# Part of level 0 moved beside the count matrix, the final sum scaled at its end, full-row bias products and a different last wait, in a graph and expert kernel

## The reference

```python
x = x + gnn(layernorm(x), src, dst)          # 625 nodes x 256, 20000 edges
x = x + ffn(layernorm(x))                    # 8 experts, the 2 best of each node, hidden size 512
# gnn: three levels, then one product over all of them
xs = [x]; h = x
for W, b in ((W0, b0), (W1, b1), (W2, b2)):
    m = concatenate([h[dst], h[src] - h[dst]]) @ W + b
    s = segment_sum(m, dst); cnt = segment_sum(1, dst)
    h = relu(s / maximum(cnt, 1)); xs.append(h)
return concatenate(xs) @ Wf + bf
```

## Time and profile before

| | us |
|---|---|
| median of three runs | 203.26 (201.93 to 204.81) |
| the profiled execution, its own time | 204.21 |
| its span | 202.4 |
| TensorE matmuls busy | 164.4 (81%) |
| VectorE busy | 100.7 (50%) |
| ScalarE busy | 70.3 (35%) |
| GpSimd busy | 69.8 (34%) |
| mean granted clock | 0.913 |

### The profile page before, as it was taken

One profiled execution on the slowest core, in us unless ns is written; L12 is line 12 of the kernel. 1 busy time (PEld: TensorE's weight loads), 2 busy tenths in 40 slices (PEclk: granted clock), 3 DMA queues, 4 the chain that ended last, 5 costly groups with the idle time before them and its releaser, 6 DMA issues.

```text
span 202.4 us, 3153 instructions
## 1 busy us (share of the span) xinstructions
PE 164.4 (81%) x1013; PEld 135.6 (67%) x1014; DVE 100.7 (50%) x259; ACT 70.3 (35%) x199; POOL 69.8 (34%) x96
## 2 busy tenths in 40 slices
PE   0443575877999999999999889996999999999700
PEld 0332354766899788989899879983676677657500
DVE  7799988784660447224534876922232232223100
ACT  7234984551400136112421076013334343433200
POOL 8506910003029075002000200005555666564560
PEclk9999995585579999999999996999999999999975
DMA  5469999500000501000000179902143235432332
GB/s 144 158 165 378 367 366 368 193 0 5 3 3 0 159 5 47 7 3 3 0 3 0 48 199 279 375 32 78 11 69 80 52 52 71 77 63 26 53 52 26
DMA packets 15784, 20.34 MB, mean 100 GB/s; under 512 B 1482, under 2 KB 12116, under 8 KB 15636
## 3 DMA queue, kind: packets, MB, share of 16 engines
q1 hardware_dynamic: 12420, 15.75, 24.2%
q0 software_dynamic: 2544, 3.54, 10.5%
q10 hardware_dynamic: 800, 0.79, 1.1%
HBM read 16.81 MB, written 3.26 MB: 99 GB/s over the span
## 4 chain that ended last, share of the span: by engine, by line
PE 66%; DVE 13%; DMA 7%; issue 4%; ACT 4%; POOL 2%; ACTq 1%; POOLq 0%; DVEq 0%
PE cnt_ps L1639 9%; PE bank L1620 5%; PE bank L1487 5%; PE cnt_ps L1338 5%; PE g_ps L1620 4%; DMA out_rows<-y_sb,row_put 4%; PE cnt_ps L1487 4%; PE bank L1331 3%; PE g_ps L1331 3%; PE g_ps L1332 3%; PE g_ps L1333 3%; DVE hot_lo L950 2%; PE bank L1333 2%; PE bank L1332 2%; DVE a_hi L1030 2%
## 5 line engine op out<-in xcount | busy, mean ns | idle before, releaser
L1639 PE MATMUL cnt_ps<-w_sb,h_t 128*128 x104 | 24.8, 381 | 2.7 <-ACT h_t L859 2.7
L1639 PEld LDWEIGHTS cnt_ps<-w_sb,h_t 128*128 128x128 f32 x104 | 18.7, 190 | 5.2 <-issue 3.2
L623 POOL DMA_INDIRECT out_rows<-y_sb,row_of x10 | 15.9, 1586 | 15.5 <-DMA out_rows<-y_sb,row_of 11.6
L617 POOL DMA_INDIRECT xg<-x_rows,row_of x12 | 12.0, 1003 | 23.4 <-DVE row_of L1297 20.1
L1379 PE MATMUL bank<-hot_key,hot_lo 125*128 125x45 bf16 (+4 forms) x80 | 8.3, 244 | 12.8 <-DVE hot_key L953 7.9
L1379 PEld LDWEIGHTS bank<-hot_key,hot_lo 125*128 125x128 bf16 x80 | 5.3, 124 | 15.4 <-DVE hot_key L953 13.2
L1273 DVE TENSOR_TENSOR y_sb<-cnt_ps,b_bc 128x256 f32<-128x256 f32 x13 | 5.5, 425 | 20.0 <-PE cnt_ps L1639 20.0
L950 DVE TENSOR_TENSOR hot_lo<-iota_lo,edge_rel 125x1024 bf16<-125x1024 int16 x20 | 14.2, 710 | 0.9 <-PE g_ps L1379 0.7
L1338 PE MATMUL cnt_ps<-ident 128*128 128x128 f32 x100 | 13.5, 297 | 0.0
L1620 PE MATMUL bank<-w_sb,xt 128*128 x28 | 13.4, 599 | 0.1
L1338 PEld LDWEIGHTS cnt_ps<-ident 128*128 128x128 f32 x100 | 12.9, 211 | 0.0
(11 more groups left out here) (279 smaller groups left out, 433.9 us busy)
## 6 DMA issues: line engine op xcount, KB each, us to landing
w_sb<-in_L_ffn_W SPq DMA_DIRECT2D x16, 512.0 KB, 10.2
b_bc<-in_L_ffn_b SPq DMA_DIRECT2D x8, 256.0 KB, 5.3
w_stage<-in_L_gnn_W SPq DMA_DIRECT2D x3, 512.0 KB, 5.6
w_stage<-in_L_gnn_Wf SPq DMA_DIRECT2D x4, 256.0 KB, 6.4
b_bc<-in_L_ffn_b SPq DMA_DIRECT2D x1, 1024.0 KB, 12.3
x_rows<-x_f ACTq DMA_DIRECT2D x1, 640.0 KB, 8.7
x_sb<-in_x SPq DMA_DIRECT2D x1, 512.0 KB
out_rows<-x_sb SPq DMA_DIRECT2D x1, 512.0 KB
```

The costliest lines, as they stand in the source:

```text
L617: pool.indirect_dma_start(out=xg[:, b, :], out_offset=None, in_=x2_rows, in_offset=bass.IndirectOffsetOnAxis(ap=rows, axis=0)).then_inc(x_ ...
L623: pool.indirect_dma_start(out=out, out_offset=bass.IndirectOffsetOnAxis(ap=rows, axis=0), in_=y_sb[:, b, :], in_offset=None, compute_op=AL ...
L1639: last = pe.matmul(bank[3][:, 0:D], h_t[:, k, :], w2_sb[:, ds(e, 1), k, :], start=k == 0, stop=k == HC - 1)
```

## The change

- In the count stage, ScalarE no longer makes `ht_f`. TensorE computes the own part of level 0 from unscaled h (`own0_product`, four parts, six products each) between the pairs; ScalarE takes it out with b0 added (`own0_out`, into `z0`; b0 comes as columns by a transfer of its own). `ys_lower` moves ahead of later pairs and additions.
- Level 0: after the degrees TensorE runs the gathered sums, then the bias and `g_product(0)` of the final sum. VectorE multiplies `z0` by the counts, adds the gathered sums and makes the lower parts. The products that spread rdeg go.
- The final sum: levels 1 to 3 add unscaled u @ Wf; level 0's part and x are added into x1 first, and the sum over u is multiplied by 1/deg when it is added. relu(u) * rdeg and its split go. `add_h` stands ahead of the gathered sums in levels 1 and 2. `Z_ORDER` and `YS_ORDER` become plain order.
- Bias products use 128 rows, the others zero. b0 is no more among them.
- `split_weights(1)` no longer waits for rdeg. `split_weights(2)` and (3) wait for `g_added` too.
- SyncE itself waits for the last scatter.

The diff, cut to its core:

```diff
-        b_rows = sb("b_rows", [BR, D], f32, gnn)
+        b_rows = sb("b_rows", [P, D], f32, gnn)
...
+            sp.dma_start(b0_col[:], B[0].rearrange("(k p) -> p k", k=KC), allow_slow_non_contiguous=True)\
+                .then_inc(b0_in, 16)
...
-            sp.wait_ge(all_scattered, 1)
+            sp.wait_ge(experts_ready, 2)
+            more = pairs(sp)
+            is_odd = odd_tile(sp)
+            for h in range(2):
+                sp.wait_ge(x_got[h], more * 16 + 16)
+            sp.wait_ge(scattered, more * 32 + is_odd * 16 + FIXED * 16)
+            sp.sem_inc(all_scattered, 1)
...
-            pool.wait_ge(rdeg_ready, 2)
             split_weights(1)
...
-                act.copy(ht_f[:, c, a:b], xn_bank(i)).then_inc(h0_copied, 1)
+            def own0_out(i):
+                cols, c = part(i)
+                act.wait_ge(own0_ps, i + 1)
+                act.activation(z0[:, c, cols], own0_bank(i), ACT.Identity, bias=b0_col[:, c:c + 1])\
+                    .then_inc(own0_ready, 1)
...
             hot_pair(16)
+            ys_lower(0, 1)
             hot_pair(17)
-            ys_lower(0, 1)
+            ys_lower(0, 2)
             add_halves(0, SPLIT_CHUNK)
-            ys_lower(0, 2)
             hot_pair(18)
+            ys_lower(0, 3)
             hot_pair(19)
-            ys_lower(0, 3)
+            ys_lower(0, 4)
             add_halves(1, CHUNKS)
-            ys_lower(0, 4)
...
+            for i in range(4):
+                scale_own0(i)
+            add_gathered(0)
+            mark(dve.tensor_tensor(diag[:], cnt_f[:].rearrange("p (t m) -> p t m", t=NT),
+                                   ident[:].unsqueeze(1).broadcast_to((P, NT, P)), ALU.mult))
+            add_gathered(1)
+            ut_lower(0, 0)
+            ut_lower(0, 1)
+            add_gathered(2)
+            wait_marked()
+            mark(dve.tensor_reduce(deg_col[:], diag[:], AX.X, ALU.add))
+            add_gathered(3)
+            ut_lower(0, 2)
+            ut_lower(0, 3)
...
+            for t in range(NT):
+                dve.tensor_tensor(x1_sb[:, t, :], g_tile(t), x_sb[:, t, :], ALU.add).then_inc(x_added, 1)
...
+                dve.scalar_tensor_tensor(x1_sb[:, t, :], g_tile(t), rdeg_col[:, t:t + 1], x1_sb[:, t, :],
+                                         ALU.mult, ALU.add).then_inc(x1_ready, 1)
...
+            sum_pair(28)
             ys_product(0, 1)
+            own0_product(0)
+            sum_pair(30)
             ys_product(0, 2)
+            sum_pair(32)
             pe.wait_ge(ys_ready, 1)
+            own0_product(1)
+            pe.wait_ge(ys_ready, 2)
             ys_product(0, 3)
+            sum_pair(34)
+            pe.wait_ge(own0_ready, 1)
+            own0_product(2)
+            sum_pair(36)
+            pe.wait_ge(ys_ready, 3)
             ys_product(0, 4)
+            sum_pair(38)
+            pe.wait_ge(own0_ready, 2)
+            own0_product(3)
...
-            for t in range(NT):
-
-                pe.matmul(g_tile(t), row_pick[:, LEVELS, :], b_split[:], start=t % 2 == 0, stop=False,
-                          skip_group_check=True)
-            for t in range(NT):
-                last = g_product(0, t)
-            last.then_inc(g_added, 1)
...
-                pe.matmul(z_bank(i), bias[:, l, m], cnt[:, cols], start=first, stop=False, skip_group_check=True)
+                pe.matmul(z_bank(i), bias[:, l - 1, m], cnt[:, cols], start=True, stop=False, skip_group_check=True)
...
                     pe.wait_ge(ys_ready, l * NT + 3)
-                    own_part(l, 1, bias, cnt, True, False)
+                    own_part(l, 3, bias, cnt)
+                    pe.wait_ge(x_added, NT)
+                    add_h(l)
                     pe.wait_ge(ys_ready, (l + 1) * NT)
-                    own_part(l, 0, bias, cnt, True, False)
-                    for i in (2, 3):
-                        gathered_sum(l, i, y_parts, a_t, False, True)
-                    if l < LEVELS - 1:
-                        add_h(l)
-                    for i in (0, 1):
-                        gathered_sum(l, i, y_parts, a_t, False, True)
+                    own_part(l, 2, bias, cnt)
+                    for i in range(4):
+                        gathered_sum(i, y_parts, a_t, False)
```

More of the change, by code:

```diff
@@ L1359, in ys_product, with own0_product, g_product @@
                 last.then_inc(ys_done, 1)
-            def g_product(l, t, hi=ht_hi, lo=ht_lo):
+            def own0_product(i):
+                cols, c = part(i)
+                m = slice(D + c * P, D + (c + 1) * P)
+                for k in range(KC):
+                    last = exact3(own0_bank(i), (w_hi[:, 0, k, m], w_lo[:, 0, k, m]),
+                                  (ht_hi[:, k, cols], ht_lo[:, k, cols]), k == 0, k == KC - 1)
+                last.then_inc(own0_ps, 1)
+            def g_product(l, t, hi, lo, first=False):
                 r, cols = l % 2, slice(t * P, (t + 1) * P)
@@ L1406, in _, with sum_pair @@
                 last.then_inc(xn_t_done, 1)
-            for u in range(20, 28):
+            def sum_pair(u):
                 sum_unit(u)
+                sum_unit(u + 1)
+            for u in range(20, 28, 2):
+                sum_pair(u)
             pe.wait_ge(w_split, 1)
@@ new lines, in level_sums @@
+                        gathered_sum(i, y_parts, a_t, True)
+                else:
+                    pe.wait_ge(ut_ready, 4 * (l - 1) + 2)
+                    own_part(l, 0, bias, cnt)
+                    own_part(l, 1, bias, cnt)
+                    for t in range(NT):
+                        if t == 1:
+                            pe.wait_ge(ut_ready, 4 * l)
+                        if t >= 3:
+                            pe.wait_ge(ys_ready, l * NT + t - 2)
+                        ys_product(l, t)
@@ L1557, in _ @@
                     pe.wait_ge(w_split, l + 1)
+                if l == 1:
+                    pe.wait_ge(cnt_read, 2)
                 with pe.If(is_general > 0):
-                    level_sums(l, [ys_hi[:].bitcast(f32), ys_lo[:].bitcast(f32)], a_f, b_level[:].bitcast(f32),
-                               cnt_f[0:BR, :])
+                    level_sums(l, [ys_hi[:].bitcast(f32), ys_lo[:].bitcast(f32)], a_f, b_level[:].bitcast(f32), cnt_f)
                 with pe.Else():
                     level_sums(l, [ys_hi, ys_lo], a_hi, b_level, cnt_r)
-            add_h(LEVELS - 1)
+                if l == 0:
+                    pe.wait_ge(b_ready, 2 + (LEVELS - 1))
+                    pe.wait_ge(own0_ready, 4)
+                    for t in range(NT):
+                        pe.matmul(g_tile(t), row_pick[:], b_split[:], start=t % 2 == 0, stop=False, skip_group_check=True)
+                    for t in range(NT):
+                        last = g_product(0, t, ht_hi, ht_lo)
+                    last.then_inc(g_added, 1)
             pe.wait_ge(w_split, LEVELS + 1)
-            for j, t in enumerate(YS_ORDER):
-                if j in (0, 2):
-                    pe.wait_ge(ht_ready, 4 * LEVELS + (4 if j else 2))
+            for t in range(NT):
+                if t in (0, 3):
+                    pe.wait_ge(ut_ready, 4 * LEVELS - (0 if t else 2))
                 g_product(LEVELS, t, ut_hi, ut_lo).then_inc(g_done, 1)
```

284 lines of the change are left out of this document (108 added, 176 removed).

## The result

| | before | after |
|---|---|---|
| median beside each other, four runs each | 204.03 us (201.93 to 205.23) | 185.30 us (185.05 to 187.13) |
| the profiled execution, its own time | 204.21 | 185.45 |
| its span | 202.4 | 183.5 |

The ratio is 0.912 (95% interval 0.908 to 0.917): faster by 8.8%. Predicted were 187.4 us, 184.5 to 192.0. Later the changed kernel was timed twice more, at 184.88 and at 186.57 us.

What follows compares the result with a forecast made beforehand. TensorE's chain was taken to bound the kernel from the degree products at 48.48 us to x1 at 112.50. Terms summed to -16.3 us, giving 187.9 from 204.21 or 187.0 from 203.26; forecast 187.4 us, range 184.5 to 192.0.

Steps and rivals of the forecast that it cites:

- Count stage, -3.1: Up to the end of the degree products: they end at 48.7 to 48.9, not 51.94; -3.1 us, bounds -4.6 and -0.5.
- rival (a): TensorE's clock falls again about 44 to 49 us through remaining gaps, costing 2.0 to 4.0 us: about 190.4; chance 0.22.
- (c): Clock rises late and own0 parts stretch the count stage by all their bound, 2 to 3 us: 190; chance 0.12.
- Level 0, -9.3: Degrees to level 1: bias -0.8, final-sum products -2.2, own parts -5.6, rdeg products -1.1, weights +0.4.
- The weights: Level 1's split on GpSimd starts near 50 us beside VectorE, ends at 59.2 with half the conflict: +0.4 us.
- an idle TensorE ahead of level 1: Before level 1: a named sign of being wrong; expected was a start at 59 right behind g_product(0), not behind GpSimd.
- rival (d): At level 0 GpSimd and VectorE block each other in full; level 1 waits 2.3 us, not 0.4: 189.3; chance 0.10.
- the one-hot row: Profile row behind the halved conflict: a 520-element one-hot took 0.95 us beside a GpSimd operation, 0.42 without.
- Bias rows, -3.0: Levels 1 and 2: 128-row bias products save 0.38 to 0.40 us in each of eight own parts; bounds 0 and -3.2.
- Rival (b): The 128-row bias products keep the gaps, so 3.0 us less gain: 190.4; chance 0.12.
- The end, -0.5: After the last scatter: SyncE waits itself, GpSimd's 0.54 us wake-up goes, last wait stays 2.4; bounds 0 and -0.6.
- The FFN stage moves as a whole: After x1: the FFN stage only shifts in time; no gain was put in the sum for routing or experts.

Runs made afterwards that it cites:

- e4: Changed kernel with the four own0 products moved from the count stage to right behind the degree products; 190.49 us, ratio 0.934 to the kernel before.
- e6: Kernel before with the new end alone, SyncE itself waiting for the last scatter; 201.36 us, ratio 0.990 to the kernel before.
- e1: Changed kernel with the bias products cut back from 128 to 36 rows; 188.06 us, ratio 0.922 to the kernel before.
- e2: Changed kernel with the old end: GpSimd waits for the last scatter and tells SyncE; 187.49 us, ratio 0.924 to the kernel before.
- e3: Changed kernel with the four scalings of z0 reading the counts from PSUM, not their SBUF copy; 186.01 us, ratio 0.913 to the kernel before.
- e8: Changed kernel with own0 part 0 behind ys_product(0, 2) and part 2 behind the last pair; 185.52 us, ratio 0.912 to the kernel before.
- e9: Changed kernel with both the count-stage order of e8 and the PSUM scalings of e3; 185.00 us, ratio 0.909 to the kernel before.
- c0: Changed kernel, unaltered, timed a second time as yardstick; 184.88 us, ratio 0.907 to the kernel before.
- e11: Changed kernel, unaltered, timed a third time; 186.57 us, ratio 0.917 to the kernel before.
- e10: e9 plus two spare TensorE products behind each of the first four transpose pairs of normalized x1; 185.48 us, ratio 0.911 to the kernel before.
- e5: Kernel before with unread spare products, six behind ys_product(0, 3) and eight behind ys_product(0, 4); 201.46 us, ratio 0.982 to the kernel before.

## Why the prediction was right

- **Count stage, -3.1: measured -3.0.** The head start was 1.15 us (pair 26 at 31.98 instead of 33.13) against 1.0, the delay by own0 part 0 a wait of 1.33 us within the bound of 1.9. The last addition ended at 48.13 us against 48.4; the other profiles of the changed kernel have 47.5 and 47.9, so the nearness to 0.1 is in part luck. By its own terms the weaker bound would have been about -1.2 and not -0.5. TensorE held the high clock over the gap in which it had fallen; e4, which takes the own parts out again, brings the fall back. e6 shows that the clock can also hold over this gap and fall behind the next wait, which the prediction did not count among the causes. So rival (a) fell, and (c) with it: the step was the short one from 37.7 us on.
- **Level 0, -9.3: measured -9.1.** The own parts, the rdeg products and the clock's share are gone as summed; e4 puts the own parts and the clock together at 5.6 us. The weights took +0.7 instead of +0.4: "an idle TensorE ahead of level 1", which the prediction had named as a sign of being wrong, did come, for 0.56 us, and level 1 started behind GpSimd and not right behind `g_product(0)`. The size stayed far from rival (d). The value taken between the ends, half, put the end of the split right within 0.1 us; the 0.5 us from there to TensorE's first product was not in the sum. And the reason for half was not right, so that it fitted is luck: the one-hot row showed an operation held up for a part of its time, while here VectorE's scalings and lower parts took more than twice their time, its diagonal (0.81 us) none more, and GpSimd's operations a third more. The split ended at 59.1 where 59.2 was forecast, having begun at 50 as forecast. Rival (d) asked for 61.4. VectorE's level 0 work ended at 60.5 us where 58 had been summed; it was hidden all the same.
- **Bias rows, -3.0, and x1, -0.4: measured -3.7.** Level 1 went from 19.07 to 17.14 us. e1 gives 2.4 us of the 3.0 back in its trace and 3.2 in its median. Rival (b) fell. What the prediction took for gaps around the short operand is, by e1, its load, which does not run beside the neighbouring products.
- **The sum up to the aggregate of x1, -15.8: measured -15.8** (115.52 to 99.72).
- **The end, -0.5: measured -1.7, the term that was mis-sized.** The step that failed is the one that took SyncE's last wait, 2.4 us, as fixed and only GpSimd's wake-up of 0.54 as gone. The 2.4 us held GpSimd's ending, 2.28 us, which started only once GpSimd had been woken; now it starts before the last scatter and SyncE's last wait is 1.3. e2 and e6 show it both ways, 1.6 and 1.7 us.
- **Not in the sum: 1.0 us in the routing stage and 0.5 in the scatters.** "The FFN stage moves as a whole" was wrong by the clock: before, it was at its lower level for 3.5 us from 122.7, after it was not. Whether this belongs to the change is open: e1, e3, e8 and e9, all near to after, have the stretch, c0, e2, e4 and e11 have not.

Against the profiled execution the sum gave 187.9 us and 185.45 were measured: 1.2 of the 2.5 us come from the end, 1.0 from the routing stage and 0.5 from the scatters, less 0.2 elsewhere.

Not undone by any run, and so read from the profiles alone: the rdeg products (-1.1), the place of `ys_lower` and the head start of the count stage, the new form of the final sum, and x1 (-0.4).

## What to carry to other kernels

Work put into TensorE's idle time can be worth twice, by its own time and by the clock that the idle time would have cost: here 5.6 us in all. Where two engines are newly put side by side, price the operations of both that read two SBUF tensors, and look again at which of them ends last. At the end of a program let an engine that has nothing left to do wait for the last transfer, and let the others end under it: 1.6 us here. A fit of the total does not prove a term: the halving of the conflict was near for a wrong reason, and the last wait was taken as fixed though nothing said what it was made of.

## What was not expected of the hardware

- The granted clock in a trace is not known before its first change, 37.3 us in after. There the window of 33 to 34 us says 1.00, but the chain steps by 0.32 us, as at the lower level:

```profile
33.00:34.00 1.00, 1.00 (x6) 0.92 (x5) 0.98 (x2) 0.22 (x2) 0.00 (x0) 1.00 1.10 362
```

```profile
36.29 0.32 PE g_ps L1334
...
37.67 0.17 PE g_ps L1336
```

  So a clock has to be checked against the step of a known product.
- A product of 36 rows between products of 128 costs 0.40 us more than one of 128 rows filled up with zeros, though its load takes the same 0.18 us.
- Taking one group of operations out of a conflict (e3) moved it to the next ones, two of 256 columns taking 2.82 us, where the group of four took 1.99 before.
- GpSimd's last long instruction took 2.28 us when it came behind the wait for the last transfer; when it stood ahead of the transfer, it was over 1.1 us behind the landing.
- Spare products are not free. In e10 they delayed the transposes by about what the high clock brought. In e5 4.1 us were gained, but 1.2 went in a wait of TensorE ahead of level 1, and with a low stretch behind it 1.75 were left at the aggregate.
